# A four-layer decoder kernel: one layer's expert tail cut into single blocks, a weight load issued earlier, two waits exchanged, two stages interleaved in another order

## The chip, the cores and the metric

The kernel runs on one core of a Trainium2 chip. The metric is the device time of one execution in microseconds (us). In the texts PE is TensorE, DVE is VectorE, ACT is ScalarE, POOL is GpSimd and SP is SyncE, which here only issues DMAs.

## The reference, cut to what matters

A decoder of four layers works on an activation of 8 sequences x 256 tokens x 512 features. Each layer has a mixing part and a feed-forward part:

```
layer 0: attention over features; then mixture of experts, top 1 of 8, capacity 256 rows each:
    xd  = zeros(8*256, 512); xd[flat] = xt            # scatter tokens to expert rows
    oe  = (silu(xd@W1) * (xd@W3)) @ W2                # each expert on its 256 rows
    out = oe[flat] * (gate*keep) + shared_expert(xt)  # gather back, scale, add
layer 1: GRU over 256 time steps; then top-1 LoRA experts on its output
layer 2: 256 time steps of a coupled oscillator, each a Runge-Kutta step of 4 evaluations:
    dq = q - q**3/3 - p + drive + tanh(q) @ coupling.T + bias ; dp = 0.08*(q + 0.7 - 0.8*p)
    then retrieval of 8x8 experts of 4096 for each token (down_embed, up_embed)
layer 3: attention and LoRA experts
```

Everything is float32 at the interfaces.

## The kernel before, in words

The activation stays in SBUF as XT (128 partitions x 4 x 2048). The program is a row of blocks; between two blocks all engines meet at a barrier. Inside a block each engine has its own list of instructions, written by hand, and semaphores order them against each other. The order in which a list is written is the order in which the engine works.

**moe0** (layer 0's experts). POOL scatters 16 blocks of 128 tokens to DRAM (L347), the eight experts run one after the other on PE (up L375, down L408), ACT stores each result (L457, L459) to DRAM as `expert_out`. When all 16 stores have landed, POOL issues 16 gathers, one for each block of 128 tokens (L354, into C0N). They all count on one semaphore, and ACT waits until it shows 256, thus all of them. Then eight rounds of a loop take two blocks each: ACT multiplies them by their gates into the small buffer m_xr (L467), PE transposes them into PSUM (L427, four transposes a block), DVE adds them to XT (L506).

**gates** loads the GRU's input weights g_wih (3 MB, L524) and two bias vectors (L525, L526) after the barrier; PE, which waits for all three (`s_w` 48), multiplies XT by g_wih (L539) while ACT adds the bias (L548) and DVE splits the recurrent weights (L558 to L562).

**scan** runs the GRU 32 steps ahead of the oscillator. After these 32 steps of GRU alone, each of 256 steps t has four evaluations k. Each evaluation on PE is 16 matmuls with low parts of weights (L620) and 16 with high parts (L624) into PSUM k_ps, then as many for one gate of the GRU (g_ps). DVE takes k_ps up in `end`: k_v (L731), then k_q (or k_qn), which ACT turns into the next k_hl (L696), which PE waits for. k_v waits for two semaphores: k_mm, from PE's last matmul, and DVE's own `dve`, from k_S a few instructions earlier.

**retrieve_experts** ends with a stage over 16 tiles of 128 tokens (here: the spread stage). For each tile i and quarter q: `scatter` on PE (L1041, 64 small matmuls from p_sel and HQ into p_up and p_sim), `spread` on ACT copies that out to r_mem (L1107, two copies a quarter), `combine` on PE (L1051, 32 matmuls) sums the tile's result from r_mem and the embeddings; the first quarter of combine waits for all four spreads of its tile. DVE makes the one-hots: pairs_hot (L1217, four a tile, each after the scatter that frees its quarter), weights_hot (L1222 and L1223, after scatter of quarter 3 of the tile before), and result (L1227), which adds the tile to XT when combine is through.

Each matmul of float32 shows as two records in the trace.

Of the kernel before, what the change touches and what calls it, by code (L numbers as in the profile page):

```python
# [66 lines left out]

def attn0(nc, K, C0T, C0N, x_nat, wqk_d, wv_d, wo_d, cond_row, pc_d):

    with ExitStack() as c:  # L70
# [3 lines left out]
        x=sb('a_x',[128,16,512]); wqk=sb('a_wqk',[128,2,2,64]); wv=sb('a_wv',[128,2,16]); wor=sb('a_wor',[128,16,256]); wos=sb('a_wos',[128,256]); pc=sb('a_pc',[128,4])  # L74
# [229 lines left out]
def moe0(nc, K, XT, s_res, C0T, C0N, wg_d, w13_d, w2a_d, w2b_d, sw13_d, sw2a_d, sw2b_d, xd, oe):  # L304
    CAP=256
    with ExitStack() as c:
        sb=lambda n,s,d=F32: c.enter_context(nc.sbuf_tensor(n,s,d)); sem=K.sem
# [8 lines left out]
        s_xr=sem('m_xr'); s_xt=sem('m_xt'); s_xtc=sem('m_xtc'); s_oe=sem('m_oe'); s_g=sem('m_g'); s_gs=sem('m_gs'); s_gt=sem('m_gt'); s_gc=sem('m_gc'); s_ws=[sem(f'm_ws{i}') for i in range(2)]  # L316
# [5 lines left out]
        def _(e):  # L322
            e.dma_start(wg[:],wg_d).then_inc(s_w,16)
            e.dma_start(w13[1][:],sw13_d).then_inc(s_wt[1],16)
# [16 lines left out]
            pair(3,True)  # L341
        @b_.gpsimd
        def _(e):
# [9 lines left out]
            for i in range(16):  # L353
                e.indirect_dma_start(C0N[:,i,:],None,oe,IND(ga[:,i:i+1],0),bounds_check=2047,oob_is_err=False).then_inc(s_g,16)  # L354
        @b_.tensor
        def _(e):
# [65 lines left out]
            with looped(e,0,8) as g:  # L422
                for j in range(2):
                    e.wait_ge(s_gs, g*2+j+1)
                    e.wait_ge(s_gc, g*2)
                    for d in range(4):
                        i=T.transpose(ps[j][:,d*128:(d+1)*128],xr[:,j,d*128:(d+1)*128],K.ident[:])  # L427
                    i.then_inc(s_gt,1)
        @b_.scalar
        def _(e):  # L430
# [18 lines left out]
            def expert(ex,last):  # L449
# [4 lines left out]
                for s in range(2):  # L454
                    e.wait_ge(s_dn,ex*2+16+s+1)
                    e.wait_ge(s_oe,ex*32)
                    A.activation(ob[:,s,:],ps[4+s][:,:],ACT.Copy).then_inc(s_dnc,1)  # L457
# [4 lines left out]
            e.wait_ge(s_g,256)
            e.wait_ge(s_xt,8)
            with looped(e,0,8) as g:
                for j in range(2):
                    e.wait_ge(s_gt,g*2)
                    A.activation(xr[:,j,:],C0N[:,g*2+j,:],ACT.Copy,scale=gk[:,bass.ds(g*2+j,1)]).then_inc(s_gs,1)  # L467
        @b_.vector
        def _(e):
# [32 lines left out]
            with looped(e,0,8) as g:  # L502
                for j in range(2):
                    e.wait_ge(s_gt,g*2+j+1)
                    dst=XT[:,:,bass.ds(g*256+j*128,128)]
                    V.tensor_tensor(dst,dst,ps[j][:,:].rearrange('p (d n) -> p d n',d=4),ALU.add).then_inc(s_gc,1)  # L506
# [5 lines left out]
def gates(nc, K, XT, GRZ, HQ, whi, wlo, chi, clo, bhn, wih_d, whh_d, bih_d, bhh_d, wT_d):  # L512

    with ExitStack() as c:
        sb=lambda n,s,d=F32: c.enter_context(nc.sbuf_tensor(n,s,d)); sem=phase_semaphores(nc,c)
        V=nc.vector; A=nc.scalar; T=nc.tensor
# [6 lines left out]
        def _(e):  # L523
            e.dma_start(wih[:],wih_d).then_inc(s_w,16)  # L524
# [6 lines left out]
        def _(e):  # L531
            e.wait_ge(s_w,48)
# [1117 lines left out]
```

## Time and profile before

| what | us |
|---|---|
| median of 3 runs | 5344.21 |
| lowest and highest run | 5337.22, 5351.23 |
| profiled execution, its own time | 5333.42 |
| span of its instructions | 5331.8 |
| PE busy, of the span | 4882.3 |
| DVE busy, of the span | 2845.8 |

The profile is of one execution; times in it count from its first instruction. A busy PE need not be at its best: in the scan PE is busy with many small matmuls. The views give a line number of the kernel before for each instruction.

### The profile page before, as it was taken

The numbers are of one execution on the slowest core, as the hardware profiler recorded it, in microseconds if no ns is written. First come the engines' busy times: TensorE is split into PE (matmuls) and PEld (weight loads), VectorE is DVE, ScalarE is ACT, GpSimd is POOL, SyncE is SP. The second block draws the span as 40 slices with busy tenths as digits, with TensorE's granted clock in tenths as the row PEclk, the third lists the DMA queues.
The fourth block names the chain that finished last, engine by engine and source line by source line (L and its number), as shares of the span: only waits on it lengthen the run. The fifth ranks groups of instructions, "written<-read, shape, count | busy, mean of one in ns | idle before, by whom it ended". The sixth has DMA issues, their size and how long they took to land. (4 is left out here: it accounts for less than half of the span.)

```text
span 5331.8 us, 197005 instructions
## 1 busy us (share of the span) xinstructions
PE 4882.3 (92%) x83712; PEld 3841.1 (72%) x83712; DVE 2845.8 (53%) x16413; ACT 1518.5 (28%) x6006; POOL 281.8 (5%) x859
## 2 busy tenths in 40 slices
PE   7899969799999999999996599999899999899978
PEld 3345644589999999999996588789899999344433
DVE  4211011378888888888887735675533331344411
ACT  1100111234444434444433222233321111333320
POOL 0010010000110101101101000000000000000000
PEclk7799989655555555555555599999989999899989
DMA  2201421000000000000001000033400000100000
GB/s 78 99 33 77 161 86 49 14 4 5 5 5 5 5 5 5 5 5 5 5 5 50 13 9 2 33 86 93 135 3 3 2 2 3 41 12 17 17 21 31
DMA packets 54335, 163.72 MB, mean 31 GB/s; under 512 B 13873, under 2 KB 18097, under 8 KB 48192
## 3 DMA queue, kind: packets, MB, share of 16 engines
q1 hardware_dynamic: 47456, 134.89, 7.6%
q8 instruction: 645, 10.57, 0.8%
q0 software_dynamic: 3712, 12.29, 0.7%
q10 hardware_dynamic: 2304, 4.20, 0.2%
q14 instruction: 218, 1.79, 0.1%
HBM read 129.63 MB, written 17.17 MB: 28 GB/s over the span
## 5 line engine op out<-in xcount | busy, mean ns | idle before, releaser
L620 PE MATMUL k_ps<-k_hl,k_wlo 128*128 128x8 f16 x16384 | 608.7, 169 | 154.8 <-ACT k_hl L696 150.2
L620 PEld LDWEIGHTS k_ps<-k_hl,k_wlo 128*128 128x128 f16 x16384 | 526.2, 105 | 239.5 <-ACT k_hl L696 175.4
L624 PE MATMUL k_ps<-k_hl,k_whi 128*128 128x16 f16 x16384 | 588.7, 174 | 0.1
L624 PEld LDWEIGHTS k_ps<-k_hl,k_whi 128*128 128x128 f16 x16384 | 516.1, 104 | 0.6 <-DVE k_lz L824 0.2
L620 PE MATMUL g_ps<-g_hl,g_wlo 128*128 128x8 f16 x12288 | 436.7, 168 | 40.9 <-DVE g_hl L774 35.8
L624 PE MATMUL g_ps<-g_hl,g_whi 128*128 128x16 f16 x12288 | 441.6, 174 | 0.0
L620 PEld LDWEIGHTS g_ps<-g_hl,g_wlo 128*128 128x128 f16 x12288 | 387.1, 104 | 47.1 <-DVE g_hl L774 41.2
L696 ACT ACTIVATE k_hl<-k_q 128x32 f16<-128x32 f32 x768 | 176.2, 229 | 782.3 <-DVE k_q L731 782.3
L624 PEld LDWEIGHTS g_ps<-g_hl,g_whi 128*128 128x128 f16 x12288 | 387.1, 104 | 0.1
L1217 DVE TENSOR_TENSOR HQ<-p_ior,p_pm 128x2048 f32<-128x2048 f32 x64 | 146.3, 2290 | 289.9 <-PE p_sim L1041 289.9
L1445 DVE TENSOR_REDUCE t_NM<-t_ps 128x1 f32<-128x512 f32 x256 | 165.0, 686 | 211.9 <-PE t_ps L1314 211.9
L1051 PE MATMUL p_dn<-r_mem,GRZ 128*128 128x128 f32 x2048 | 249.7, 285 | 16.3 <-ACT r_mem L1107 16.3
L1051 PE MATMUL p_pq<-r_mem,GRZ 128*128 128x128 f32 x2048 | 248.5, 285 | 16.3 <-ACT r_mem L1107 16.3
L731 DVE SCALAR_TENSOR_TENSOR k_v<-k_ps,k_S 128x32 f32<-128x32 f32 x1024 | 195.7, 191 | 118.7 <-PE k_ps L624 115.9
L1051 PEld LDWEIGHTS p_dn<-r_mem,GRZ 128*128 128x128 f32 x2048 | 243.6, 200 | 18.2 <-ACT r_mem L1107 17.2
L1051 PEld LDWEIGHTS p_pq<-r_mem,GRZ 128*128 128x128 f32 x2048 | 243.0, 200 | 18.1 <-ACT r_mem L1107 17.2
L480 DVE TENSOR_TENSOR m_hT<-m_sA,m_ps 128x256 f32<-128x256 f32 (+1 forms) x72 | 36.6, 509 | 386.1 <-ACT m_sA L441 386.1
L983 PE MATMUL p_up<-HQ,GRZ 128*128 128x256 f32 x1024 | 225.2, 382 | 2.0 <-PEq L22 2.0
L824 DVE CUSTOM_DVE_ANT_1 k_hl<-k_T,k_hl 128x32 f16<-128x32 f32 x1024 | 197.0, 192 | 50.3 <-ACT k_T L697 7.6
L699 ACT ACTIVATE k_sq<-k_q 128x32 f32<-128x32 f32 x1024 | 218.1, 213 | 0.0
L983 PEld LDWEIGHTS p_up<-HQ,GRZ 128*128 128x128 f32 x1024 | 196.4, 192 | 29.4 <-issue 2.1
L1107 ACT ACTIVATE r_mem<-p_up 128x512 f32<-128x512 f32 x64 | 68.4, 1069 | 518.8 <-PE p_sim L1041 518.8
(321 smaller groups left out, 9034.5 us busy)
## 6 DMA issues: line engine op xcount, KB each, us to landing
GRZ<-expert_places SPq DMA_DIRECT2D x64, 512.0 KB, 4.9
m_w<-in_w_dram SPq DMA_DIRECT2D x8, 2816.0 KB, 10.3
m_w<-in_w2a_dram SPq DMA_DIRECT2D x8, 1280.0 KB, 12.7
GRZ<-in_ue_dram SPq DMA_DIRECT2D x8, 1024.0 KB, 7.8
XT<-in_xT_dram SPq DMA_DIRECT2D x1, 4096.0 KB, 12.4
a_x<-in_x_nat_dram SPq DMA_DIRECT2D x4, 1024.0 KB, 18.1
expert_rows<-m_zero SPq DMA_DIRECT2D x1, 4096.0 KB, 23.5
m_xr<-expert_rows POOLq DMA_DIRECT2D x8, 512.0 KB, 4.0
```

What stands on the lines that cost most here:

```text
L480: V.tensor_tensor(hT[0:M,m,0:n],sA[0:M,st,0:n],ps[st*2+1][0:M,0:n],ALU.mult).then_inc(s_h,1)
L620: T.matmul(P[:,j,1,:],lo[:,kc,(m0+j)*128:(m0+j+1)*128],x[:,kc,0,:],start=(j==0 and kc==0),stop=False,skip_group_check=True)
L624: i=T.matmul(P[:,j,:,:],hi[:,kc,(m0+j)*128:(m0+j+1)*128],x[:,kc,:,:],start=False,stop=kc==KC-1,skip_group_check=True)
L696: A.activation(kl[:,:,0,:],m4(src),ACT.Tanh).then_inc(k_hi,1)
L699: A.activation(sq[:],q[:,k,:],ACT.Square).then_inc(k_sq,1)
L731: stt=lambda o,x,y,z: V.scalar_tensor_tensor(o,x,y,z,ALU.mult,ALU.add)
L824: V.tensor_tensor_reduce(kl[:,:,1,:],m4(Tt[:]),kl[:,:,0,:],S,0.0,ALU.subtract,ALU.max,lz[:,0:1]).then_inc(k_lo,1)
L983: x=T.matmul(psu[n%2][:,(m%2)*256:(m%2+1)*256],wup[:,dd,m*128:(m+1)*128],HQ[:,dd,s*256:(s+1)*256],start=dd==0,stop=dd==3)
L1051: x=T.matmul(pso[i%2][:,dd*128:(dd+1)*128],ue[:,cc,dd*128:(dd+1)*128],Ws[i%2][:,cc,:],start=cc==0 and dd==0,stop=cc==31,skip_group_check=True)
L1107: A.activation(Ws[i%2][:,:,b*64+q*16:b*64+q*16+16].rearrange('p c j -> p j c'),psw[b][n%2][:,:].rearrange('p (j c) -> p j c',c=32),ACT.Cop ...
L1217: V.tensor_tensor(Bp[:,q],bc(ior[:].unsqueeze(1),[128,16,128]),bc(PM[:,i,1,q*16:(q+1)*16].unsqueeze(2),[128,16,128]),ALU.is_equal).then_in ...
L1445: V.tensor_reduce(NM[:,qc,hh*64+32:hh*64+33],psX[hh][:,:],AX.X,ALU.max,negate=True).then_inc(s_mx,1)
```

## The change

Four things change; the rest of the difference moves buffers in SBUF (C0T becomes HQ, C0N and attn0's x become parts of GRZ, and a buffer `wm` of 128 x 6144 serves as expert weights, then as the GRU's input weights, then as LoRA weights and as half of r_mem), with no instruction added by it.

1. The tail of moe0 is written out in 16 single blocks: each gather has a semaphore of its own, ACT scales block g in place when gather g has landed, PE transposes it into one of four PSUM banks, DVE adds it.
2. The load of the GRU's input weights is issued in moe0, when expert 6 is through (`s_dn` 30); PE in gates waits for it alone, DVE for the two biases.
3. In scan's `end` the wait for k_mm is written ahead of the wait for k_S.
4. In the spread stage `scatter(i+1,q)` stands ahead of `combine(i,q)`, and DVE's `result(i)` behind weights_hot(i+2) and the last pairs_hot.

```diff
@@ moe0 @@
+            e.wait_ge(s_dn,30)
+            e.dma_start(wm.rearrange('p (d n) -> p d n',d=4),wih_d).then_inc(s_gw,16)
...
             for i in range(16):
-                e.indirect_dma_start(C0N[:,i,:],None,oe,IND(ga[:,i:i+1],0),bounds_check=2047,oob_is_err=False).then_inc(s_g,16)
+                e.indirect_dma_start(C0N[:,i,:],None,oe,IND(ga[:,i:i+1],0),bounds_check=2047,oob_is_err=False).then_inc(s_g[i],16)
...
-            with looped(e,0,8) as g:
-                for j in range(2):
-                    e.wait_ge(s_gs, g*2+j+1)
-                    e.wait_ge(s_gc, g*2)
-                    for d in range(4):
-                        i=T.transpose(ps[j][:,d*128:(d+1)*128],xr[:,j,d*128:(d+1)*128],K.ident[:])
-                    i.then_inc(s_gt,1)
+            for g in range(16):
+                e.wait_ge(s_gs,g+1)
+                if g>=4: e.wait_ge(s_gc,g-3)
+                for d in range(4):
+                    i=T.transpose(ps[g%4][:,d*128:(d+1)*128],C0N[:,g,d*128:(d+1)*128],K.ident[:])
+                i.then_inc(s_gt,1)
...
-            e.wait_ge(s_g,256)
-            e.wait_ge(s_xt,8)
-            with looped(e,0,8) as g:
-                for j in range(2):
-                    e.wait_ge(s_gt,g*2)
-                    A.activation(xr[:,j,:],C0N[:,g*2+j,:],ACT.Copy,scale=gk[:,bass.ds(g*2+j,1)]).then_inc(s_gs,1)
+            for g in range(16):
+                e.wait_ge(s_g[g],16)
+                A.activation(C0N[:,g,:],C0N[:,g,:],ACT.Copy,scale=gk[:,g:g+1]).then_inc(s_gs,1)
@@ gates @@
-            e.dma_start(wih[:],wih_d).then_inc(s_w,16)
...
-            e.wait_ge(s_w,48)
+            e.wait_ge(s_gw,16)
@@ scan @@
             def end(t,k):
                 P=view(psk[k%2])
+                e.wait_ge(k_mm,t*4+k+1)
                 ch.after(at['S'])
-                e.wait_ge(k_mm,t*4+k+1)
@@ retrieve_experts @@
                 for q in range(4):
+                    scatter(i+1,q)
                     combine(i,q)
-                    scatter(i+1,q)
...
                 for q in range(3): pairs_hot(4*i+8+q)
-                result(i)
                 weights_hot(i+2)
                 pairs_hot(4*i+11)
+                result(i)
```

How the instructions stand. DVE in the scan, one evaluation; the names in brackets are the semaphores waited for, in the order in which the built program has them: where there are two, the first is waited for by an instruction of its own ahead, the second by the instruction itself. Before:

```order
L731 SCALAR_TENSOR_TENSOR k_X<-k_q,k_X 128x32 [waits dve]
L731 SCALAR_TENSOR_TENSOR k_W<-k_q,k_W 128x32
L731 SCALAR_TENSOR_TENSOR k_v<-k_ps,k_S 128x32 [waits k_mm,dve]
L731 SCALAR_TENSOR_TENSOR k_q<-k_ps,k_v 128x32 [waits dve]
L731 SCALAR_TENSOR_TENSOR k_pn<-k_q,k_W 128x32 [waits dve,k_q]
L731 SCALAR_TENSOR_TENSOR k_X<-k_q,k_X 128x32
L758 TENSOR_TENSOR g_t<-g_r,g_hn 128x32 [waits dve,g_sr]
```

And of the change:

```order
L727 SCALAR_TENSOR_TENSOR k_X<-k_q,k_X 128x32 [waits dve]
L727 SCALAR_TENSOR_TENSOR k_W<-k_q,k_W 128x32
L727 SCALAR_TENSOR_TENSOR k_v<-k_ps,k_S 128x32 [waits dve,k_mm]
L727 SCALAR_TENSOR_TENSOR k_q<-k_ps,k_v 128x32 [waits dve]
L727 SCALAR_TENSOR_TENSOR k_pn<-k_q,k_W 128x32 [waits dve,k_q]
L727 SCALAR_TENSOR_TENSOR k_X<-k_q,k_X 128x32
L754 TENSOR_TENSOR g_t<-g_r,g_hn 128x32 [waits dve,g_sr]
```

No instruction moved; in k_v alone the two waits have changed places (g_t, for comparison, has its second wait for ACT in both).

PE at the end of moe0 and the beginning of gates; before it is a loop over two banks:

```order
L422 BRANCH_PREFETCH_HINT
L422 ISA
L427 MATMUL m_ps<-ident,m_xr 128x128 x4
L424 REGISTER_ALU
L427 MATMUL m_ps<-ident,m_xr 128x128 x4
L422 REGISTER_ALU
L422 COMPARE_AND_BRANCH
L306 UNCONDITIONAL_BRANCH
```

And of the change:

```order
L410 MATMUL m_ps<-m_w,m_hT 128x512 x12
L428 MATMUL m_ps<-ident,GRZ 128x128 x64
L306 UNCONDITIONAL_BRANCH
L526 UNCONDITIONAL_BRANCH
L529 UNCONDITIONAL_BRANCH
```

The 64 transposes are the same in number and now stand in one line without a loop, reading the gathered block itself.

DVE in the spread stage, one tile (p_sel is written by weights_hot, HQ by pairs_hot, XT by result). Before:

```order
L1227 TENSOR_TENSOR XT<-XT,p_dn 128x4x128
L1222 TENSOR_TENSOR p_sel<-p_ior,p_pm 128x2048
L1223 TENSOR_TENSOR p_sel<-p_sel,p_pm 128x2048
L1217 TENSOR_TENSOR HQ<-p_ior,p_pm 128x2048 x4
L1227 TENSOR_TENSOR XT<-XT,p_pq 128x4x128
```

And of the change:

```order
L1213 TENSOR_TENSOR HQ<-p_ior,p_pm 128x2048 x3
L1218 TENSOR_TENSOR p_sel<-p_ior,p_pm 128x2048
L1219 TENSOR_TENSOR p_sel<-p_sel,p_pm 128x2048
L1213 TENSOR_TENSOR HQ<-p_ior,p_pm 128x2048
L1223 TENSOR_TENSOR XT<-XT,p_pq 128x4x128
L1213 TENSOR_TENSOR HQ<-p_ior,p_pm 128x2048 x3
```

The result's addition has moved behind three instructions of 2048 columns, to the end of the tile's work on DVE.

## Rows read from the trace of the kernel before

**Rows 1.** The page: its first line.

```profile
span 5331.8 us, 197005 instructions
```

**Rows 2.** Window of the scan: us, busy us and (instructions) of each engine, PEclk, DMA share, GB/s.

```profile
1124.00:3060.00 1936.00, 1780.97 (x54984) 1695.50 (x54982) 1680.48 (x13523) 755.00 (x4744) 193.51 (x767) 0.50 0.03 8
```

**Rows 3.** Timeline, 770 to 808 us: start, length, instruction, [idle before <-releaser].

```profile
771.99 1.33 ACT L467 ACTIVATE m_xr<-C0N,m_gk 128x512 f32 x2 [27.17 <-DMA C0N<-expert_out,m_ga]
...
774.03 0.69 DVE L506 TENSOR_TENSOR XT<-XT,m_ps 128x512 f32 x1 [41.06 <-PE m_ps L427]
...
795.33 0.69 DVE L506 TENSOR_TENSOR XT<-XT,m_ps 128x512 f32 x1 [0.17 <-PE m_ps L427]
796.30 0.34 SPq L524 DMA_DIRECT2D g_wih<-in_wih_dram  x1
...
807.22 1.22 PE L539 MATMUL w_ps<-XT,g_wih 128*128 x1 [12.04 <-DMA g_bhh<-in_bhh_dram]
```

**Rows 4.** Lines L347 and L354: durations ns min/median/max, first and last start.

```profile
L347 POOL DMA_INDIRECT expert_rows<-C0N,m_sc x16: 974/976/1229, 284.1 to 303.6; - x16
...
L354 POOL DMA_INDIRECT C0N<-expert_out,m_ga x16: 997/1002/1094, 747.7 to 767.4; - x16
...
DMA to landing us min/median/max: 3.4/3.7/4.2
```

**Rows 5.** Timeline, first steps of the scan, 1000 to 1003 us.

```profile
999.96 0.60 PE L624 MATMUL g_ps<-g_hl,g_whi 128*128 128x16 f16 x16
...
1000.60 0.19 DVE L731 SCALAR_TENSOR_TENSOR g_b<-g_ps,g_bhn 128x32 f32<-128x32 f32 x1 [0.69 <-PE g_ps L624]
...
1001.92 0.23 ACT L673 ACTIVATE g_r<-g_ar 128x32 f32<-128x32 f32 x1 [2.24 <-DVE g_ar L731]
1002.18 0.19 DVE L758 TENSOR_TENSOR g_t<-g_r,g_hn 128x32 f32<-128x32 f32 x1 [0.29 <-ACT g_r L673]
```

**Rows 6.** Timeline, one evaluation in the scan, 2503 to 2506 us.

```profile
2503.76 0.57 PE L624 MATMUL k_ps<-k_hl,k_whi 128*128 128x16 f16 x16
...
2504.44 0.19 DVE L731 SCALAR_TENSOR_TENSOR k_v<-k_ps,k_S 128x32 f32<-128x32 f32 x1 [0.18 <-PE k_ps L624]
2504.59 0.50 PEld L624 LDWEIGHTS g_ps<-g_hl,g_whi 128*128 128x128 f16 x16
...
2505.18 0.51 PEld L620 LDWEIGHTS k_ps<-k_hl,k_wlo 128*128 128x128 f16 x16
```

**Rows 7.** Timeline, the same stretch: k_v and what stands ahead of it.

```profile
2506.15 0.18 DVE L766 TENSOR_TENSOR g_d<-g_HS,g_n 128x32 f32<-128x32 f32 x1
...
2506.31 0.19 DVE L731 SCALAR_TENSOR_TENSOR k_v<-k_ps,k_S 128x32 f32<-128x32 f32 x1
...
2507.98 0.18 DVE L731 SCALAR_TENSOR_TENSOR k_Q<-k_G,k_Q 128x32 f32<-128x32 f32 x1
2508.08 0.18 DVE L731 SCALAR_TENSOR_TENSOR k_B<-k_G,k_AQ 128x32 f32<-128x32 f32 x1
2508.20 0.19 DVE L731 SCALAR_TENSOR_TENSOR k_v<-k_ps,k_S 128x32 f32<-128x32 f32 x1
```

**Rows 8.** Timeline of PE, two combines of the spread stage.

```profile
3913.03 7.41 PE L1051 MATMUL p_dn<-r_mem,GRZ 128*128 128x128 f32 x64
...
3924.50 9.04 PE L1051 MATMUL p_pq<-r_mem,GRZ 128*128 128x128 f32 x64 [2.05 <-ACT r_mem L1107]
```

**Rows 9.** Line L1051, the combines: durations, starts, and idle time before them.

```profile
L1051 PE MATMUL p_dn<-r_mem,GRZ x2048: 274/275/582, 3883.1 to 4494.1; 128*128 128x128 f32 x187
...
its engine sat idle before it (us, times) until:
  ACT r_mem L1107: 67.1, 32
```

**Rows 10.** Timeline of DVE, where the spread stage begins.

```profile
3883.48 2.29 DVE L1223 TENSOR_TENSOR p_sel<-p_sel,p_pm 128x2048 f32<-128x2048 f32 x1
```

**Rows 11.** Window of the second of these combines, columns as in rows 2.

```profile
3924.50:3933.50 9.00, 9.00 (x68) 8.88 (x68) 4.80 (x3) 0.00 (x0) 0.00 (x0) 0.81 0.01 2
```

More of the change, by code:

```diff
@@ L61, in _, with attn0 @@
             G.affine_select(out=K.tri[:],in_=K.tri[:],compare_op=ALU.is_ge,fill=0.0,base=0,pattern=[[1,128]],channel_multiplier=-1)
-def attn0(nc, K, C0T, C0N, x_nat, wqk_d, wv_d, wo_d, cond_row, pc_d):
+def attn0(nc, K, C0T, C0N, side, x_nat, wqk_d, wv_d, wo_d, cond_row, pc_d):
     with ExitStack() as c:
@@ L73, in attn0 @@
         NP=4
[L74 removed]
+        x=side.rearrange('p (i n) -> p i n',n=512); wqk=sb('a_wqk',[128,2,2,64]); wv=sb('a_wv',[128,2,16]); wor=sb('a_wor',[128,16,256]); wos=sb('a_wos',[128,256]); pc=sb('a_pc',[128,4])
         cm=sb('a_cm',[128,4,512]); CB=sb('a_CB',[128,512]); warm=sb('a_warm',[128,8])
@@ L296, in route_bufs, with moe0 @@
     return r
-def moe0(nc, K, XT, s_res, C0T, C0N, wg_d, w13_d, w2a_d, w2b_d, sw13_d, sw2a_d, sw2b_d, xd, oe):
+def moe0(nc, K, XT, s_res, C0T, C0N, side, wm, s_gw, wih_d, wg_d, w13_d, w2a_d, w2b_d, sw13_d, sw2a_d, sw2b_d, xd, oe):
     CAP=256
@@ L315, in moe0 @@
         s_up=sem('m_up'); s_silu=sem('m_silu'); s_h=sem('m_h'); s_dn=sem('m_dn'); s_dnc=sem('m_dnc')
-        s_xr=sem('m_xr'); s_xt=sem('m_xt'); s_xtc=sem('m_xtc'); s_oe=sem('m_oe'); s_g=sem('m_g'); s_gs=sem('m_gs'); s_gt=sem('m_gt'); s_gc=sem('m_gc'); s_ws=[sem(f'm_ws{i}') for i in range(2)]
+        s_xr=sem('m_xr'); s_xt=sem('m_xt'); s_xtc=sem('m_xtc'); s_oe=sem('m_oe'); s_g=[sem(f'm_g{i}') for i in range(16)]; s_gs=sem('m_gs'); s_gt=sem('m_gt'); s_gc=sem('m_gc'); s_ws=[sem(f'm_ws{i}') for i in range(2)]
         V=nc.vector; A=nc.scalar; T=nc.tensor
@@ L501, in _, with gates @@
             with looped(e,0,8) as ex: dvexp(ex)
[L502 to L512, printed above, removed]
+            for g in range(16):
+                e.wait_ge(s_gt,g+1)
+                dst=XT[:,:,g*128:(g+1)*128]
+                V.tensor_tensor(dst,dst,ps[g%4][:,:].rearrange('p (d n) -> p d n',d=4),ALU.add).then_inc(s_gc,1)
+def gates(nc, K, XT, GRZ, HQ, wih, s_gw, whi, wlo, chi, clo, bhn, whh_d, bih_d, bhh_d, wT_d):
     with ExitStack() as c:
@@ L566, with scan @@
 LEAD, TL = 32, 16
-def scan(nc, K, XT, GRZ, HQ, whi, wlo, chi, clo, bhn, cond_d, bias_d, wb_d, bb_d, ar_d, bw_d, wup, wdn, wup_d, wdn_d, s_pw):
+def scan(nc, K, XT, GRZ, HQ, wm, whi, wlo, chi, clo, bhn, cond_d, bias_d, wb_d, bb_d, ar_d, bw_d, wup, wdn, wup_d, wdn_d, s_pw):
     with ExitStack() as c:
@@ L608, in _ @@
             e.dma_start(bi[:],bias_d).then_inc(s_c,16)
-            for t,dr in ((ar,ar_d),(wb,wb_d),(bw,bw_d),(bb,bb_d)): e.dma_start(t[:],dr).then_inc(s_lw,16)
+            for t,dr in ((ar,ar_d),(wb,wb_d),(bw,bw_d),(bb[:],bb_d)): e.dma_start(t,dr).then_inc(s_lw,16)
             e.wait_ge(g_h,NT)
@@ L1569, in decoder_layers @@
         with ExitStack() as c1:
-            C0T=c1.enter_context(nc.sbuf_tensor('C0T',[128,4,2048],F32)); C0N=c1.enter_context(nc.sbuf_tensor('C0N',[128,16,512],F32))
-            attn0(nc,K,C0T,C0N,x_nat,wqk0,wv0,wo0,cond,pc0)
-            moe0(nc,K,XT,s_x,C0T,C0N,wg,w13,w2a,w2b,sw13,sw2a,sw2b,xd,oe)
-        with ExitStack() as c1:
             HQ=c1.enter_context(nc.sbuf_tensor('HQ',[128,4,8,256],F32))
@@ L1578, in decoder_layers @@
                 flat=GRZ[:].rearrange('p m b t -> p (m b t)')
+                C0T=HQ[:].rearrange('p d b t -> p d (b t)'); C0N=flat[:,0:8192].rearrange('p (i n) -> p i n',n=512); side=flat[:,8192:16384]
+                attn0(nc,K,C0T,C0N,side,x_nat,wqk0,wv0,wo0,cond,pc0)
+                wm=c2.enter_context(nc.sbuf_tensor('wm',[128,6144],F32)); s_gw=K.sem('s_gw')
+                moe0(nc,K,XT,s_x,C0T,C0N,side,wm[:],s_gw,wih,wg,w13,w2a,w2b,sw13,sw2a,sw2b,xd,oe)
                 wup_s=flat[:,0:8192].rearrange('p (d n) -> p d n',d=4); wdn_s=flat[:,8192:12288].rearrange('p (c n) -> p c n',c=16)
@@ L1583, in decoder_layers @@
                     whi=sb('g_whi',[128,4,1536],F16); wlo=sb('g_wlo',[128,4,1536],F16); chi=sb('k_whi',[128,4,512],F16); clo=sb('k_wlo',[128,4,512],F16); bhn=sb('g_bhn',[128,32])
-                    gates(nc,K,XT,GRZ,HQ,whi,wlo,chi,clo,bhn,wih,whh,bih,bhh,couplingT)
-                    scan(nc,K,v4(XT),GRZ,HQ,whi,wlo,chi,clo,bhn,cond32,bias32,wb,bb,ar1,bw1,wup_s,wdn_s,wup,wdn,s_pw)
+                    gates(nc,K,XT,GRZ,HQ,wm[:].rearrange('p (d n) -> p d n',d=4),s_gw,whi,wlo,chi,clo,bhn,whh,bih,bhh,couplingT)
+                    scan(nc,K,v4(XT),GRZ,HQ,wm[:],whi,wlo,chi,clo,bhn,cond32,bias32,wb,bb,ar1,bw1,wup_s,wdn_s,wup,wdn,s_pw)
                 QT=HQ[:].rearrange('p d b t -> p d (b t)')
-                retrieve_experts(nc,K,XT,QT,flat,s_pw,rows,bup,bdn,wq,keys,deT,ue)
+                retrieve_experts(nc,K,XT,QT,wm[:],flat,s_pw,rows,bup,bdn,wq,keys,deT,ue)
             attn3(nc,K,XT,QT,wq3,wo3,cond,pc,rd)
```

32 lines of the change are left out of this document (16 added, 16 removed).

## The prediction

> **What bounds the kernel now.** I read the page first: one core, a span of 5331.8 us [rows 1]. Then a window by stage. The scan fills 1936 us of it, with PE at a granted clock of 0.50, the lower of its two levels (1.2 GHz) [rows 2]; the spread stage's combines run from 3883 to beyond 4494 us [rows 9]. Then the timeline, at the four places that the change touches, to see which wait ends last there.
>
> At the end of moe0 nothing works but POOL: it issues 16 gathers, the first at 747.7, the last at 767.4 us, thus one each 1.31 us, and each lands 3.4 to 4.2 us after its issue [rows 4]. ACT waits until the last has landed and starts at 771.99; DVE's 16 additions then run from 774.03 to 795.33 + 0.69 = 796.02, one each 1.42 us [rows 3]. Then the barrier; SP issues the 3 MB of weights at 796.30, and PE starts at 807.22, 11.20 us behind the last addition, having waited for DMA [rows 3].
>
> In the scan the work goes in a ring: PE's last matmul, k_v, k_q, ACT, PE again. k_v starts 2504.44 - (2503.76 + 0.57) = 0.11 us after PE's matmuls end, and PE's loads pause from 2504.59 + 0.50 = 2505.09 to 2505.18 [rows 6]. So PE has 0.09 us of slack in an evaluation, and the ring sets the pace.
>
> In the spread stage PE is the one that others wait for, but it idles 67.1 us in 32 entries, half for matmuls and half for their weight loads, so 33.5 us in 16 waits of 2.1, on ACT's spreads [rows 9]. The combine behind such a wait takes 9.04 us where another takes 7.41 [rows 8]; the mean clock in it is 0.81, so part of it ran at the lower level [rows 11].
>
> **Moe0's tail.** The sixteen gathers and their issue stay. Each block now goes on when it has landed. The last lands by 767.4 + 4.2 = 771.6 at most, and what follows it is one block through ACT, PE and DVE: from ACT's start to the first addition's end took 774.03 + 0.69 - 771.99 = 2.73 us [rows 3]. This gives an end at 774.7. It needs the earlier blocks to keep up. Their cadence is 1.31 us, an addition takes 0.69, ACT's two scalings 1.33 together. Even if the old pace of 1.42 a block stayed, beginning from a first landing at 747.7 + 3.4 = 751.1, the last addition would end at 751.1 + 2.73 + 15 x 1.42 = 775.1. Gain: 796.0 - 774.7 = 21.3 us, 20.9 by the slower bound. The DVE additions now run beside POOL's issuing, which they did not before. POOL's row shows 0.997 to 1.094 us an issue with DVE idle, and the scatters' issues 0.974 to 1.229 earlier in the stage [rows 4]. The Trainium skill, "SBUF — State Buffer", section "Who interferes with whom", says that DVE and GpSimd share one pair of ports, which locks one of them out for a whole instruction, but that a DVE instruction with at most one SBUF input outside the two-port modes does not contend. These additions read one input from PSUM. No row here shows them side by side with gathers.
>
> **Weights ahead.** PE's 11.20 us between the last addition and its first matmul shrink to the barrier. SP's issue comes 0.28 us after the addition's end [rows 3]; that is the lower bound. I take 0.5, and 3 as the upper bound. Gain 10.7 (8.2 to 10.9). The load itself is issued during expert 7 and has over 60 us there. Small DMAs of the biases hide under PE's first group. PE starts gates at the lower clock before as after, so I charge nothing. Tail and load together: 32.0.
>
> **The exchanged waits.** Before, k_mm, the late one, is waited for by an instruction of its own ahead of k_v; after, it stands on k_v, and the early one (k_S, which stands three instructions and more ahead of k_v in DVE's list) stands ahead. What is the place worth? In the first 32 steps g_b, which waits for PE's same kind of group through one wait on itself, starts 1000.60 - (999.96 + 0.60) = 0.04 us after it [rows 5]; k_v takes 0.11 [rows 6]. And g_t, with two waits of which the late one (ACT's) stands on it, starts 1002.18 - (1001.92 + 0.23) = 0.03 us after ACT [rows 5]. So two waits cost nothing when the late one is second, and the place is worth 0.07 us. "Perfetto Trace Analysis" of the Trainium skill, section "Identifying Dependency Chains", says as much of the form: extra waits may be inserted as instructions of their own ahead.
>
> DVE's list limits what can be taken. In evaluation k=0, k_B starts at 2508.08 and k_v at 2508.20; in k=3, g_d at 2506.15 and k_v at 2506.31 [rows 7]. k_Q and k_B ahead of it show that DVE's instructions follow each other by 0.10 [rows 7], so 0.02 can be gained at k=0 and 0.05 at k=3; 0.07 at k=1 and k=2, where k_v's wait for PE is the longer [rows 6]. Sum 0.21 a step, x 256 = 53.8 us. Bounds: 0.07 at all 1024 evaluations is 71.7; and since PE has only 0.09 of slack, and its expert matmuls of layer 1 fall into k=3, I put the low bound at 0.12 a step, 30 us. Queued behind k_v are k_q and the rest of DVE's list, which come earlier with it.
>
> **The spread stage.** The wait of 2.05 us before combine(i,0) goes, since combine(i-1,3) with its 7.41 us and the next scatter now stand between scatter(i,3) and combine(i,0), and ACT's spread fits under it. With the wait the slow beginning of that combine goes, 9.04 - 7.41 = 1.63 [rows 8]: combines that follow a scatter without a wait run at 7.41. This makes 3.68 us for each of 15 tiles, 55.2. The first tile pays: scatter(1,0) stands ahead of combine(0,0) and needs weights_hot(1), which ends at 3883.48 + 2.29 = 3885.77 [rows 10]. A scatter takes 3924.50 - 2.05 - (3913.03 + 7.41) = 2.0 us [rows 8], so combine(0,0) starts at 3887.8 and not at 3883.1 [rows 9], 4.7 later, less the 2.0 of the scatter that it has done by then: 2.7. Gain 52.5. New waits: scatter(i+2,0) needs weights_hot(i+2), 2 x 2.29 = 4.6 us after scatter(i+1,3), under combine(i,3)'s 7.41; the pairs_hot behind it makes 6.9 us. result(i) waits for combine(i,3) at the end of DVE's tile, with nothing urgent behind it. If the clock's dips stayed without the wait, the gain would be 15 x 2.05 - 2.7 = 28.
>
> **Sum.** 32.0 + 53.8 + 52.5 = 138.3 us. From the profiled execution's own 5333.4 this gives 5195; that execution lies 10.8 below the median of the runs shown, which is what is asked, so 5344.2 - 138.3 = 5206. The moved buffers add no instruction and I charge nothing for them.
>
> **The rivals.**
> - The place of the wait is worth nothing, because k_v's 0.11 us come from something else, say its reading of two inputs. Then 84.5 us are gained: 5260. For it: g_b also reads PSUM but in another place of the program. Against it: 0.04 beside 0.11 for the same group of PE and the same kind of instruction [rows 5, 6].
> - The spread stage gives half or nothing: DVE becomes late with weights_hot(i+2) or the dips stay. Without 52.5 it is 5258, with 28 it is 5230. Against it: 4.6 under 7.41.
> - POOL's issues are held up by the additions, 16 x 0.69 = 11 us at most: 5217. This is the rule of the shared ports in case it held for these additions; the Trainium skill's page exempts them.
> - Slower: k_v comes late by its new first wait. DVE must see its own k_S, then take up k_v; if this ended after PE's signal in each evaluation, all 1024 would be longer. The other parts save 84.5 us, so it decides from (84.5 + 16) / 1024 = 0.10 us an evaluation on; at 0.12 it is 5382. Against it: the three or more instructions between k_S and k_v take 0.10 us each [rows 7].
>
> **How the numbers follow.** Forecast, all parts work: 0.77. No gain from the wait: 0.09. Spread stage at half or nothing: 0.08. POOL held: 0.03. Slower by the wait: 0.03. The range reaches from all bounds at their best (71.7 + 52.5 + 32 gives 5188, less some us of scatter among runs) to the two rivals near 5258: 5178 to 5255. 0.3% is 16 us, about what a measurement of this kernel can tell from no change. Faster takes in all cases but the last: 0.96; within 0.3%: 0.02, a mild form of the last; slower: 0.02.
>
> **What would show it.** ACT's first scaling near 751 and DVE's last addition of moe0 near 775; PE's first matmul of gates within 1 us of it. In the scan k_v 0.04 us behind PE in evaluations 1 and 2, and a step of 1936 / 256 - 0.21 = about 7.35 us [rows 2]. In the spread stage no idle time of PE behind ACT from the second tile on, and no combine of 9 us. I am wrong if the k_v gap stays 0.11, if PE's own work takes up the slack, or if PE waits for p_sel in the spread stage.

## The result

The changed kernel takes 5215.9 us (median of 4 runs, 5213.9 to 5227.6), the kernel before, run beside it on the same chip, 5347.7 (5337.2 to 5354.3). The ratio is 0.9763, with a 95% interval of 0.9748 to 0.9777: 127 us less (119 to 135 with the interval's ends); the two medians themselves differ by 132. The forecast was 5206, 138 us less than before. One execution of the kernel before, in the session of the first experiments below, took 7326 us at a granted clock of 0.53; it counts in no ratio.

The profiled execution of the changed kernel is the slowest of its four (5227.6), that of the kernel before was faster than all four of its runs (5333.4), so their spans differ by 106 us only. The page's first line, which answers to [rows 1]:

```profile
span 5225.8 us, 196853 instructions
```

I cut both traces at six marks, and did so for every later kernel too (us; "first gather" is its issue on POOL):

| stretch | before | changed |
|---|---|---|
| start to first gather of moe0 | 747.7 | 763.0 |
| first gather to end of last addition | 48.3 | 26.5 |
| last addition to PE's first matmul of gates | 11.2 | 0.8 |
| from there to the first k_v of the scan | 317.0 | 319.6 |
| first k_v to last k_v | 1932.6 | 1877.5 |
| last k_v to end of last combine | 1471.9 | 1421.3 |
| from there to the end | 803.1 | 817.1 |

The four stretches that the change aims at give 21.8 + 10.4 + 55.1 + 50.6 = 137.9 us. The first and the last take 15 and 14 us back in this pair of executions, and gates with the lead 2.6. In the last no instruction changed; the first has the new issue of the weight load at its end, and its instructions use moved buffers.

**Moe0's tail.** The timeline of the changed kernel, which answers to [rows 3]:

```profile
766.50 0.72 ACT L465 ACTIVATE GRZ<-GRZ,m_gk 128x512 f32<-128x512 f32 x1 [6.42 <-DMA GRZ<-expert_out,m_ga]
...
788.80 0.69 DVE L503 TENSOR_TENSOR XT<-XT,m_ps 128x512 f32<-128x512 f32 x1 [1.05 <-PE m_ps L428]
...
790.26 1.21 PE L535 MATMUL w_ps<-XT,wm 128*128 x1 [1.50 <-PEq L306]
```

And the row of the gathers, which answers to [rows 4]:

```profile
L356 POOL DMA_INDIRECT GRZ<-expert_out,m_ga x16: 994/998/1091, 763.0 to 782.7; - x16
```

ACT starts 3.5 us after the first gather's issue (766.50 - 763.01) and not 24.3; the last addition ends at 788.80 + 0.69 = 789.49, 6.8 us behind the last issue. The issues take 0.994 to 1.091 us as in [rows 4] with DVE idle, though 12 of DVE's 16 additions now overlap an issue in time: POOL was not held. PE's first matmul of gates comes at 790.26, 0.77 us behind the last addition.

**The scan.** A window answers to [rows 2] and has its columns:

```profile
1110.00:2988.00 1878.00, 1738.31 (x54969) 1700.49 (x54966) 1664.37 (x13519) 755.46 (x4744) 191.94 (x764) 0.50 0.03 8
```

The timeline answers to [rows 6, 7]:

```profile
2001.18 0.57 PE L620 MATMUL k_ps<-k_hl,k_whi 128*128 128x16 f16 x16
...
2001.79 0.19 DVE L727 SCALAR_TENSOR_TENSOR k_v<-k_ps,k_S 128x32 f32<-128x32 f32 x1
```

PE's matmuls end at 2001.18 + 0.57 = 2001.75 and k_v starts at 2001.79: 0.04 us in place of 0.11. PE's busy time is 43 us less (1738 against 1781 in [rows 2]) with the same matmuls: part of the ring's waiting is shown as busy time of PE, and the idle columns alone would not have found it. Only the k_v of k=3 (2005.40) stands further behind PE, whose matmuls end at 2004.76 + 0.57 = 2005.33 (the row is shown further down).

**The spread stage.** The combines' line answers to [rows 9]:

```profile
L1047 PE MATMUL p_dn<-wm,GRZ x2048: 274/275/580, 3820.4 to 4379.8; 128*128 128x128 f32 x187
...
its engine sat idle before it (us, times) until:
```

Nothing stands behind the colon there. The timeline of PE has the first scatter of this order, the only one that waits, and the first combine, the only slow one:

```profile
3816.82 0.32 PE L1037 MATMUL p_up<-p_sel,HQ 64*64 64x32 f32 x2 [4.72 <-DVE p_sel L1219]
...
3820.39 8.65 PE L1047 MATMUL p_dn<-wm,GRZ 128*128 128x128 f32 x64
```

The stage's window has the columns of [rows 2]:

```profile
3820.39:4408.70 588.31, 588.30 (x11652) 578.59 (x11648) 201.59 (x99) 119.27 (x120) 0.00 (x0) 1.00 0.01 3
```

No idle time before a combine any more; PE is busy in 588.30 of 588.31 us at a granted clock of 1.00 (2.4 GHz). The same stretch before had 0.96 and took 645.6.

### The profile page after: what moved, and what is told of

It is laid out like the page before. It is cut to its first block and busy times, and to the rows that moved or that the text cites. A ratio compares the mean times of both kernels' runs of the same rounds, so it can differ in the third digit from the quotient of the medians.

```text
span 5225.8 us, 196853 instructions
## 1 busy us (share of the span) xinstructions
PE 4851.0 (93%) x83712; PEld 3836.6 (73%) x83712; DVE 2831.0 (54%) x16413; ACT 1520.9 (29%) x6006; POOL 280.7 (5%) x859
## 5 line engine op out<-in xcount | busy, mean ns | idle before, releaser
L616 PE MATMUL g_ps<-g_hl,g_wlo 128*128 128x8 f16 x12288 | 436.7, 168 | 43.2 <-DVE g_hl L770 38.2
L478 DVE TENSOR_TENSOR m_hT<-GRZ,m_ps 128x256 f32<-128x256 f32 (+1 forms) x72 | 36.6, 509 | 385.2 <-ACT GRZ L442 385.2
L1047 PE MATMUL p_dn<-wm,GRZ 128*128 128x128 f32 x2048 | 238.4, 277 | 0.0
L1047 PE MATMUL p_pq<-r_mem,GRZ 128*128 128x128 f32 x2048 | 236.3, 276 | 0.0
L1047 PEld LDWEIGHTS p_dn<-wm,GRZ 128*128 128x128 f32 x2048 | 232.3, 193 | 1.3
L1047 PEld LDWEIGHTS p_pq<-r_mem,GRZ 128*128 128x128 f32 x2048 | 230.9, 192 | 1.1
L820 DVE CUSTOM_DVE_ANT_1 k_hl<-k_T,k_hl 128x32 f16<-128x32 f32 x1024 | 197.0, 192 | 49.0 <-ACT k_T L693 6.6
L823 DVE SCALAR_TENSOR_TENSOR k_g<-k_sq,k_q 128x32 f32<-128x32 f32 x1024 | 194.8, 190 | 0.0
## 6 DMA issues: line engine op xcount, KB each, us to landing
wm<-in_w_dram SPq DMA_DIRECT2D x4, 2816.0 KB, 10.4
```

The costliest lines, as they stand in the source:

```text
L616: T.matmul(P[:,j,1,:],lo[:,kc,(m0+j)*128:(m0+j+1)*128],x[:,kc,0,:],start=(j==0 and kc==0),stop=False,skip_group_check=True)
L820: V.tensor_tensor_reduce(kl[:,:,1,:],m4(Tt[:]),kl[:,:,0,:],S,0.0,ALU.subtract,ALU.max,lz[:,0:1]).then_inc(k_lo,1)
L823: at['g']=ch.did(V.scalar_tensor_tensor(g[:],sq[:],-3.0,q[:,k,:],ALU.add,ALU.mult))
L1047: x=T.matmul(pso[i%2][:,dd*128:(dd+1)*128],ue[:,cc,dd*128:(dd+1)*128],Ws[i%2][:,cc,:],start=cc==0 and dd==0,stop=cc==31,skip_group_check=True)
```

## The experiments

The marks of all profiled executions, in us; "same" stands for a length within 0.5 of the changed kernel's, or 1.7 in the stretch of the spread. Times are medians, ratios are to the kernel before with their intervals.

| kernel | time | ratio | gather to last addition | to gates' PE | scan | last k_v to last combine |
|---|---|---|---|---|---|---|
| before | 5342 to 5348 | | 48.3 | 11.2 | 1932.6 | 1471.9 |
| changed | 5215.9 | 0.9763 [0.9748, 0.9777] | 26.5 | 0.8 | 1877.5 | 1421.3 |
| wait_undone | 5263.0 | 0.9853 [0.9837, 0.9869] | same | same | 1933.2 | same |
| spread_undone | 5264.9 | 0.9853 [0.9832, 0.9874] | same | same | 1880.4 | 1473.1 |
| tail_undone | 5219.3 | 0.9764 [0.9746, 0.9782] | 36.3 | same | same | same |
| load_late | 5217.6 | 0.9768 [0.9750, 0.9786] | same | 11.0 | 1878.2 | same |
| before_wait | 5289.6 | 0.9910 [0.9893, 0.9927] | 48.0 | 11.1 | 1877.7 | 1472.8 |
| wait_k0 | 5224.8 | 0.9788 [0.9770, 0.9806] | same | same | 1892.1 | same |
| wait_k3 | 5220.8 | 0.9772 [0.9754, 0.9789] | same | same | 1888.2 | same |
| spread_result | 5332.1 | 0.9978 [0.9963, 0.9993] | same | same | same | 1541.5 |
| best | 5232.2 | 0.9792 [0.9770, 0.9813] | same | same | 1898.9 | 1417.7 |
| nb_late | 5235.7, one run | | same | same | 1890.9 | 1419.6 |
| tail_2banks | 5230.8, one run | | 38.2 | same | 1876.5 | 1419.0 |
| first_tile | 5205.6 | 0.9745 [0.9731, 0.9758] | 27.1 | same | 1878.0 | 1416.9 |

Medians scatter by some 5 to 10 us, as tail_undone and load_late show; a stage's length scatters by 1 to 3. For edits worth 5 to 15 us I go by the stage.

**Undo one part each**, all four on one chip.

```diff
@@ wait_undone @@
-                e.wait_ge(k_mm,t*4+k+1)
                 ch.after(at['S'])
+                e.wait_ge(k_mm,t*4+k+1)
@@ spread_undone @@
-                    scatter(i+1,q)
                     combine(i,q)
+                    scatter(i+1,q)
...
+                result(i)
                 weights_hot(i+2)
                 pairs_hot(4*i+11)
-                result(i)
@@ tail_undone @@
+            for g in range(16): e.wait_ge(s_g[g],16)
             for g in range(16):
-                e.wait_ge(s_g[g],16)
                 A.activation(...)
@@ load_late: the dma_start of wih_d stands at the head of gates @@
```

> The changed kernel with the two waits of k_v as before (k_S first, k_mm, from PE, second in the code). Theory (the late wait on an instruction of its own costs 0.07 us, as far as DVE's list leaves it): the scan gets its 55 us back, 5216 -> 5270, and k_v starts 0.11 us behind PE again; the other stages stay. If the place of the wait is worth nothing, and the scan's gain came from where the buffers lie: 5216 +- 8. If the place is worth 0.07 in all 1024 evaluations: 5288.

Measured: the scan is 1933.2, +55.7, and k_v stands 0.107 us behind PE (median, 0.108 at k=0), in none of the 1024 evaluations less than 0.105, where the changed kernel has 0.039, 0.038, 0.038 and 0.057 for k = 0 to 3. The first theory holds; buffers have no part in it. The other way round, the kernel before with this edit alone:

> The kernel before with one edit: k_mm is waited for first in the code, k_S second. Theory (the place of the late wait alone makes the scan's gain): first to last k_v 1932.6 -> 1877.5, so 5346 - 55 = 5291, and nothing moves in moe0 or the spread stage. If the moved buffers had a part in it: less than 55, down to 0.

Measured: the scan 1877.7, -54.9, the rest as before, the time 5289.6. The exchange makes the whole gain of the scan, whatever else is changed.

> The changed kernel with the spread stage's order as before (combine(i,q) ahead of scatter(i+1,q), result(i) ahead of weights_hot(i+2)). Theory (16 waits of 2.05 us and 16 slow combines of 9.04 us come back, less 2.7 in the first tile): 5216 + 51 = 5267, combines behind the wait at about 9 us. If the slow combine has nothing to do with the wait: 5216 + 28 = 5244. If the moved buffers made the gain: 5216 +- 8.

Measured: last k_v to last combine 1473.1, +51.8, the waits and the slow combines back. The timeline of PE, one such combine of spread_undone:

```profile
3849.89 9.04 PE L1047 MATMUL p_pq<-r_mem,GRZ 128*128 128x128 f32 x64 [2.06 <-ACT r_mem L1103]
```

> The changed kernel, but ACT waits for all sixteen gathers before its first scaling; the rest (single blocks without a loop, four banks, load ahead) stays. Theory (the gain is that the blocks pass while the later gathers are issued): the last addition ends about 48 us less the loop's own cost behind the first gather's issue; with 16 blocks at the pace of one addition and its wait (0.8 to 1.0 us) in place of 1.42, 24 + 2.7 + 15 x 0.9 = 40 against 26.5 now, thus +13.7, 5230; at the old pace of 1.42 it is +21.8, 5238. If the four banks alone had made the gain: +0 to 3.

Measured: 36.3 us, +9.8, below both of my figures. Once all gathers have landed, the sixteen blocks now pass in 9.9 us of ACT (row below, timeline of tail_undone), and DVE's additions, which start from 785.65 to 795.65, follow each other by 0.67 us in the mean, faster than the 0.9 I had taken. The time itself, 5219, doesn't tell this from nothing.

```profile
783.73 9.91 ACT L465 ACTIVATE GRZ<-GRZ,m_gk 128x512 f32<-128x512 f32 x16 [26.61 <-DMA GRZ<-expert_out,m_ga]
```

Part of that pace is PE's clock. The first five additions stand 0.86 us apart, the later ones 0.60, and two windows of tail_undone (columns of [rows 2]) have PE at a granted clock of 0.54 and then of 1.00:

```profile
783.70:789.50 5.80, 5.00 (x26) 5.00 (x27) 3.18 (x5) 5.77 (x10) 0.00 (x0) 0.54 0.00 0
789.50:796.30 6.80, 5.21 (x41) 4.04 (x38) 6.80 (x12) 4.14 (x7) 0.00 (x0) 1.00 0.00 0
```

PE works without a pause from 784.50 to the end of the first window (5.00 us busy). In the kernel before and in the changed one, where it pauses between blocks, its clock is 0.50, the lower level, through the whole tail. At 0.86 us throughout, the fifteen steps would have taken 12.8 us and not 10.0, so some 2.8 us of the form's gain are the clock's (an estimate from these distances).

So of the 21.8 us of the tail, 12.0 were won by the new form of the loop alone (48.3 - 36.3), and the separate gathers give the other 9.8 on top of it. Which piece of the form does it was the next question: tail_undone with `ps[g%2]` and a wait two blocks back in place of `ps[g%4]` and four.

> The changed kernel, with ACT waiting for all sixteen gathers as in tail_undone and only two PSUM banks for the transposes, without a loop. tail_undone took 36.3 us from the first gather's issue to the last addition's end, the kernel before 48.3. If the banks made these 12 us: 48. If the loop and the small buffer m_xr, which held ACT until PE had read it, made them: 36 to 38.

Measured: 38.2. The second pair of banks is worth 1.9 us; some 10 come from what is left: the loop, the buffer m_xr, which ACT could only fill again when PE had read both halves, and PE's higher clock (in tail_2banks 0.58 up to 789.50 and then 1.00). These I did not separate. The timeline of the kernel before shows the buffer's wait, ahead of each pair of blocks:

```profile
774.89 1.34 ACT L467 ACTIVATE m_xr<-C0N,m_gk 128x512 f32 x2 [1.57 <-PE m_ps L427]
```

Seven such waits of 1.57 to 1.59 us make 11 us, in which ACT and PE take turns.

> The changed kernel with the GRU's input weights loaded after the barrier, at the head of gates. Theory: PE waits 11.2 us again behind the last addition in place of 0.8, 5216 + 10.4 = 5226. If the load under expert 7 had slowed that expert by its DMA traffic, part of it is given back: less than 10.

Measured: 11.0 us to PE's first matmul, +10.2, as expected. The other stages stay, and the time of 5217.6 hides it.

**Where in the step the gain of the waits lies.** The wait order of before in one evaluation only:

```diff
             def end(t,k):
                 P=view(psk[k%2])
+                if k==0: ch.after(at['S'])
                 e.wait_ge(k_mm,t*4+k+1)
-                ch.after(at['S'])
+                if not (k==0): ch.after(at['S'])
```

(and with 3 for 0 in wait_k3).

> The changed kernel with the old order of waits in evaluation k=0 only. In the changed kernel's trace k_v of k=0 starts 0.038 us behind PE in the 11 of 16 steps that hold expert matmuls of layer 1, and 0.112 in the other 5, where DVE's list holds it. Theory (PE's gap comes back where the list doesn't hold k_v, and nothing absorbs it, since k=0's matmuls are what is waited for): 11/16 x 0.069 x 256 = +12 us in the scan, 5228. If k=0 is worth only what I gave it in the prediction, 0.02: +5, 5221. If it were worth 0.07 in all steps: +18.

> The changed kernel with the old order of waits in evaluation k=3 only. k_v of k=3 starts 0.057 us behind PE in the changed kernel and 0.107 in the old order. Theory (in the 11 of 16 steps with expert matmuls PE itself comes 0.06 us late to the next k=0, so that an earlier k_v of k=3 gives nothing there): 5/16 x 0.05 x 256 = +4 us, 5220, and PE's first matmul of k=0 goes from 0.116 to about 0.066 us behind k_hl. If gains of the evaluations simply add, as my prediction had it: 0.05 x 256 = +13, 5229.

Measured: +14.6 us for k=0 and +10.7 for k=3. The medians of the steps, taken from the records of each trace (us; "with" are the steps in which PE has expert matmuls of layer 1 between k=3 and the next k=0; by the records they are 180 of the 256 steps, namely 12 of each 16 but none of the last 16, where my expectations took 11 of 16, thus 176; the theory's +12 for k=0 stands):

| | before | changed | wait_k0 | wait_k3 |
|---|---|---|---|---|
| PE's first matmul of k=0 behind k_hl, with | 0.058 | 0.119 | 0.123 | 0.058 |
| k_v of k=0 behind PE, with | 0.107 | 0.038 | 0.108 | 0.082 |
| k_v of k=0 behind PE, without | 0.112 | 0.111 | 0.109 | 0.108 |
| k_v of k=3 to k_v of k=0, with | 1.894 | 1.879 | 1.952 | 1.869 |

For k=0 the theory holds: nothing absorbs the gap. For k=3 it falls. PE's lateness did go, from 0.119 to 0.058, but DVE's list behind the later k_v of k=3 then held the next k_v (0.082 in place of 0.038), so that the stretch to k=0 shrank by 0.010 and not by 0.05. PE's expert matmuls and DVE's list of k=0 bound the same evaluation within hundredths; relief on one alone is worth little. The changed kernel's timeline shows the first bound:

```profile
2004.03 0.23 ACT L692 ACTIVATE k_hl<-k_q 128x32 f16<-128x32 f32 x1 [0.49 <-DVE k_q L727]
...
2004.32 0.58 PE L616 MATMUL k_ps<-k_hl,k_wlo 128*128 128x8 f16 x16
...
2004.76 0.57 PE L620 MATMUL k_ps<-k_hl,k_whi 128*128 128x16 f16 x16
...
2005.19 1.20 PE L644 MATMUL l_pso<-g_HS,wm 128*128 128x128 f32 x4
...
2005.40 0.18 DVE L727 SCALAR_TENSOR_TENSOR k_v<-k_ps,k_S 128x32 f32<-128x32 f32 x1
...
2005.84 0.23 ACT L692 ACTIVATE k_hl<-k_qn 128x32 f16<-128x32 f32 x1 [0.20 <-DVE k_qn L727]
...
2006.18 0.61 PE L616 MATMUL k_ps<-k_hl,k_wlo 128*128 128x8 f16 x16
```

k_hl is ready at 2005.84 + 0.23 = 2006.07, PE's first matmul on it starts at 2006.18, 0.11 later; one evaluation earlier, without the experts, 2004.32 follows 2004.03 + 0.23 by 0.06.

**The DVE half of the spread edit.** scatter(i+1,q) stays ahead, result(i) goes back ahead of weights_hot(i+2).

> The changed kernel with result(i) ahead of weights_hot(i+2) again, scatter(i+1,q) still ahead of combine(i,q). Theory (this half of the edit is what lets the other half work): weights_hot(i+2) now starts only after combine(i,3), and scatter(i+2,0), which stands right behind it on PE, waits 0.7 + 2 x 2.29 + 0.1 = 5.4 us for it, in 14 tiles: +75 us, 5291, slower in this stage than before; slow combines may add up to 1.6 us for each such wait (+23). If DVE's order didn't matter: 5216.

Measured: 1541.5, +120 us, slower there than before. The wait is as expected, 5.3 us; the slow work behind it was under-priced. Timeline of PE, spread_result, the wait:

```profile
3902.30 0.32 PE L1037 MATMUL p_up<-p_sel,HQ 64*64 64x32 f32 x2 [5.31 <-DVE p_sel L1219]
```

The scatter behind the wait runs from 3902.30 to 3905.93, 3.63 us in place of 2.07, and the combine after it takes 8.63 in place of 7.41, in the next tile 9.71, and so by turns. With the wait that is 8.1 and 9.2 us a tile, seven times each, 121 in all. The window of that scatter and of the combine behind it (columns of [rows 2]):

```profile
3902.30:3905.86 3.56, 3.56 (x128) 3.50 (x128) 2.14 (x1) 0.00 (x0) 0.00 (x0) 0.50 0.02 5
3905.86:3914.49 8.63, 8.63 (x72) 8.51 (x71) 2.29 (x1) 1.95 (x2) 0.00 (x0) 0.85 0.00 0
```

The scatter runs at a granted clock of 0.50, the lower level, the combine behind it at 0.85, a later one, of 7.41 us, at 1.00.

**A better version.** Three edits: the first tile with combine(0,0) ahead of scatter(1,0), g_d (`diff(s)`) behind end(t,3), and k_B (`n_B`) behind end(t,0).

```diff
-                    scatter(i+1,q)
-                    combine(i,q)
+                    if i==0 and q==0: combine(i,q); scatter(i+1,q)
+                    else: scatter(i+1,q); combine(i,q)
...
-                e.wait_ge(k_aq,t*2+2)
-                n_B=ch.did(stt(B0[:,0,:],G0[:],-h*a*EPS*(1-kap),AQ[:,0,:]))
                 end(t,0)
+                e.wait_ge(k_aq,t*2+2)
+                n_B=ch.did(stt(B0[:,0,:],G0[:],-h*a*EPS*(1-kap),AQ[:,0,:]))
...
-                diff(s)
                 end(t,3)
+                diff(s)
```

> The changed kernel with three edits: combine(0,0) ahead of scatter(1,0) in the first tile alone; in the scan g_d (diff) behind end(t,3) and k_B behind end(t,0). Theory: the first combine starts 4.7 us earlier (spread stage -4.7); in evaluation k=0 DVE's list no longer holds k_v in the 5 of 16 steps without expert matmuls, 5/16 x 0.07 x 256 = -5.6; k=3's k_v comes 0.02 earlier, worth -1.5 where PE's expert matmuls don't absorb it. Together -12: 5204. If what was moved only makes k_hl's low part late behind ACT, the scan stays at 1877.5 or grows by up to 0.1 us a step (+25).

> The changed kernel with k_B alone behind end(t,0). Theory: k_v of k=0 starts 0.04 us behind PE in all steps, first to last k_v 1877.5 -> 1872; g_d's place in k=3 unchanged. If k_B, then ahead of three others before k_hl's low part, makes that late: 1877.5 to 1903.

Measured: the scan is longer, 1898.9 and 1890.9. With k_B moved, k_v of k=0 does stand 0.038 behind PE in nearly every step (within 0.045 in 237 of 256, in the changed kernel in 168), and the stretch from k=3 to k=0 loses 0.074 us in the 76 steps without experts. But k_hl's low part (L820, the custom instruction) starts 0.99 us behind k_v of k=0 and not 0.83, behind k_B in DVE's list; PE waits for it between its two groups, and the stretch from k=0 to k=1 grows from 1.793 to 1.873 (medians of all 256 steps). That is 20.5 us lost against 5.6 won. g_d behind end(t,3) does the same one evaluation on: low part of the next k=0 at 0.94 in place of 0.83, 1.893 in place of 1.875. So only the first edit was kept:

> The changed kernel with combine(0,0) ahead of scatter(1,0) in the first tile alone. Theory: PE's first combine no longer waits for weights_hot(1); the stage from the last k_v to the last combine goes from 833.0 + 588.3 to about 4 us less, as in best, where it was 1417.7; all else stays: 5212. That is less than the runs scatter by, so the stage's length decides, not the time.

Measured: 1416.9 from last k_v to last combine, -4.4, as in best (1417.7). The time is 5205.6, 10 us below the changed kernel's median; some 4 of them are the edit's, the rest lies in the stretches that no edit touches. It is the fastest kernel of the study, by an amount of its own that only the stage shows.

## Why the prediction was right

The direction and the place of each gain were as forecast; 127 us came of 138.

- **Moe0's tail**, 21.3 forecast, 21.8 in the trace. The size was right, but I put it all down to the blocks that go on as gathers land. The runs show that without that 12.0 of it are there, because the new form moves a block in 0.67 us where the old one took 1.42. With the early start the blocks come at POOL's 1.3 us an issue, and a faster pace has little left to gain. The old pace with the early start, which I had priced at 20.9, was not run, so how far the early start alone would reach is not shown. A slip that changes little: 771.6 + 2.73 is 774.3; the 774.7 comes from ACT's start at 771.99.
- **Weights ahead**, 10.7 forecast, 10.4 seen and 10.2 in load_late. PE's start was 0.77 us behind the addition, not 0.5.
- **The exchanged waits**, 53.8 forecast, 55.1 seen, 55.7 and 54.9 by the two experiments. The comparison with g_b and g_t of the same trace [rows 5] gave the price, 0.07 us, to the hundredth. For k=3 [rows 7] give 2506.31 - 2506.15 - 0.10 = 0.06 and not the 0.05 that I wrote, thus 0.22 a step and 56 us. The division over the step held too: I had 0.02, 0.07, 0.07 and 0.05 for k = 0 to 3, and the median stretch that ends at each k_v shrank by 0.020 (1.894 to 1.874), 0.073, 0.074 (1.867 to 1.793) and 0.056 (1.867 to 1.811). But at k=0 the size came out partly by luck: DVE's list holds k_v only in the 76 steps without expert matmuls; in the other 180 the gap did shrink by 0.069 and PE's expert matmuls took 0.05 of it back at the group's beginning. I had named these matmuls only for a low bound of the price. Nor are the terms independent: undone alone, k=0 is worth 14.6 / 256 = 0.057 a step and not 0.02.
- **The spread stage**, 52.5 forecast, 50.6 seen and 51.8 in spread_undone. From the first combine on, 57.3 came for 57.2 (the 55.2 of my 15 tiles and the 2.0 of the scatter done early), with some luck: the slow combines of before took 9.04 us in the first two of these tiles and 8.89 to 8.96 in the others, while the first combine fell from 9.30 to 8.65. The mis-sized term is the first tile: combine(0,0) starts 6.7 us later and not 4.7. Scatter(1,0), behind PE's idle 4.72 us, took 3.57 us (3816.82 to 3820.39, at a granted clock of 0.50) where I had taken 2.0 from a scatter with no wait ahead of it. first_tile recovers 4.4 us of the stage.
- **What is missing** from 138 are some 11 us by the ratio (127, 119 to 135 with its interval) and 6 by the medians. The stages give 137.9 in the traces, so no step of the sum failed. The first and last stretches account for the difference in the profiled pair. Among the twelve profiled executions with the changed buffers, the same instructions took 746.7 to 763.0 us up to the first gather (three near 747, nine from 757 on) and 801.3 to 818.8 behind the last combine. The whole difference in the first stretch lies ahead of moe0's first scatter: from that scatter to the first gather all fourteen profiled executions took 463.6 or 463.7 us, eleven of them with the weight load issued in it, so the load costs nothing there. Up to the scatter the five executions with a granted clock of 0.80 took 283.0 to 284.1 us (before, before_wait, wait_undone, load_late, first_tile), the nine with 0.75 or 0.76 took 293.3 to 299.4. A window of load_late over part of attn0 (columns of [rows 2]):

```profile
60.00:250.00 190.00, 159.59 (x513) 65.76 (x510) 66.29 (x71) 34.40 (x61) 5.05 (x4) 0.77 0.19 71
```

The same window of the changed kernel:

```profile
60.00:250.00 190.00, 159.86 (x488) 65.69 (x486) 66.28 (x71) 34.29 (x61) 5.05 (x4) 0.68 0.19 71
```

The granted clock was 0.77 in one execution and 0.68 in the other, in work in which they don't differ. The clock is thus the likeliest source of the scatter among one kernel's runs. The two profiled executions with the old buffers (before and before_wait) have 747.7 and 747.2 up to the first gather and 803.1 and 803.0 at the end, where the twelve have 757 and 810 in the mean. That would be 9 and 7 us, more than is missing. But both were quick executions of their kernels: the kernel before has 5333.4 in its profiled one and up to 5357 in the others that count, before_wait 5278.2, the lowest of its six, and up to 5299.9. So longer executions come with the old buffers too, though none of them was traced. It stays open whether the moved buffers make them more frequent; I made no run with the buffers alone moved.

Of the rivals, the place of the wait worth nothing fell by wait_undone; spread at half fell by its window (no slow combine but the first); POOL held fell by its row; a late k_v fell by the gap of 0.04. PE waiting for p_sel, named as what would make me wrong, happens in the first tile alone, where the forecast had charged it; spread_result shows what the new order of PE costs without that of DVE.

## What to carry to other kernels

Where an instruction waits for two semaphores, write the wait that comes last so that it stands on the instruction (in this program that was the one written first), and price it by a pair in the same trace that already has it. It is worth nothing where the list ahead is as late as the signal. When two edits serve one wait (early start and faster pace), price them together: here their gains would not add, by my figure of 20.9 for the one, which no run shows, beside 12.0 for the other and 21.8 for both. And when two engines are equally late, relief on one is absorbed by the other. Moving an instruction behind a critical one only helps if what follows on that engine has room: look at the next instruction that another engine waits for.

## What the runs showed of the hardware

- A satisfied early wait ahead and the late one on the instruction: 0.038 us from PE's last matmul to DVE's start (664 of the changed kernel's 1024 evaluations within 0.045; the others are held by DVE's list or another instruction). The late one on a separate instruction ahead: 0.107, and at least 0.105 in all 1024 evaluations of before and of wait_undone.
- After a wait of 2.05 us a combine took 8.9 to 9.04 us in place of 7.41. After one of 4.72 us (changed kernel, first tile) the scatter took 3.57 in place of 2.07 and the combine behind it 8.65; after one of 5.31 (spread_result) 3.63 and 8.6 to 9.7. An idle stretch of TensorE thus costs in this stage some 1.5 us beyond itself, and 2.7 to 3.9 for the longer ones.
- In tail_undone, where PE's transposes began without pauses between them, the granted clock was 0.54 in the window up to 789.50 and 1.00 in the next, and DVE's additions came 0.86 us apart at first and 0.60 then. In the kernel before and the changed one, where PE waited between blocks, it stayed at 0.50.
- The granted clock of the same instructions early in the program differs between executions (0.68 and 0.77 in one window of 190 us), and the time up to the first gather with it, from 746.7 to 763.0 us; behind the first scatter of moe0 the executions no longer differ (463.6 or 463.7 us to the first gather in all fourteen).
